# All four chunks of the soma product laid between the groups of the span phase

## What is computed

```python
# layer 0: per-language adapter
h = relu(x @ W1 + b1); x = x + layernorm(x + h @ W2 + b2) * gamma0 + beta0
# layer 1
ctx    = causal_ema(x, tau_ctx)
wg     = sigmoid(concat([x, ctx]) @ Wg.T + bg)          # "wg", the gates
gated  = x * wg                                          # g
mod    = 0.5 + sigmoid(gelu(x @ Wn1.T + bn1) @ Wn2.T + bn2)   # 8 factors per token
traces = [causal_ema(gated * mod[d], tau[d]) for d in range(8)]
temporal = sum_d traces[d] * softmax(blend)[d]
gate = sigmoid(temporal @ Wtemp.T + btemp)
soma = gelu(x @ Wsoma.T + bsoma)                         # "soma"
out  = (soma * gate) @ Wout.T
x = x + layernorm(out) * gamma1 + beta1
```

## Time and profile before

| what | us |
|---|---|
| median of three runs | 1395.28 |
| lowest and highest of them | 1391.39, 1396.88 |
| the profiled execution, its own time | 1391.26 |
| its span in the trace | 1389.3 |
| PE busy | 1345.3 (97% of the span) |
| DVE busy | 1019.6 (73%) |
| ACT busy | 511.2 (37%) |
| POOL busy | 379.0 (27%) |
| time of the packets of q1, share of 16 DMA engines | 45.9% |

### The profile page before, as it was taken

One profiled execution on the slowest core, in us unless ns is written; L12 is line 12 of the kernel. 1 busy time (PEld: TensorE's weight loads), 2 busy tenths in 40 slices (PEclk: granted clock), 3 DMA queues, 4 the chain that ended last, 5 costly groups with the idle time before them and its releaser, 6 DMA issues.

```text
span 1389.3 us, 19545 instructions
## 1 busy us (share of the span) xinstructions
PE 1345.3 (97%) x7836; PEld 971.2 (70%) x7836; DVE 1019.6 (73%) x1499; ACT 511.2 (37%) x804; POOL 379.0 (27%) x295
## 2 busy tenths in 40 slices
PE   4799999999999999999999999999999999999998
PEld 2657768677686767768577686767868677686766
DVE  7987777786777777777786777767777786677565
ACT  3225234242523425244242433425234252433412
POOL 3614123041420504123031322304123041330202
PEclk9899999999999999999999999999999999999999
DMA  7373451826438172461715626074451825426061
GB/s 261 121 194 118 121 171 63 208 84 163 141 89 222 38 215 81 126 210 58 209 44 152 190 76 197 31 192 150 114 160 68 210 94 143 161 72 172 25 158 61
DMA packets 91483, 186.21 MB, mean 134 GB/s; under 512 B 9858, under 2 KB 14594, under 8 KB 87298
## 3 DMA queue, kind: packets, MB, share of 16 engines
q1 hardware_dynamic: 91394, 184.98, 45.9%
HBM read 134.61 MB, written 50.33 MB: 133 GB/s over the span
## 4 chain that ended last, share of the span: by engine, by line
PE 57%; DMA 12%; DVE 11%; issue 8%; ACT 3%; SPq 2%; POOL 2%; DVEq 0%; POOLq 0%
PE ring L919 40%; DMA g_blocks<-g_f 7%; PE Tp L1093 5%; DMA grep<-g_blocks 5%; DVE U L825 4%; PE ring L912 3%; PE Tp L1102 3%; SPq L331 2%; PE ring L1114 2%; PE Tp L919 1%; DVE x L755 1%; DVE V L760 1%; ACT U L500 1%; DVE g_f L834 1%; PE ring L939 1%
## 5 line engine op out<-in xcount | busy, mean ns | idle before, releaser
L825 DVE TENSOR_TENSOR U<-grep,w_qs 128x1024 f32<-128x1024 f32 x256 | 300.8, 1220 | 74.4 <-DMA grep<-g_blocks 35.7
L385 POOL TENSOR_TENSOR x<-grep,b_row 128x512 f32<-128x512 f32 x64 | 80.7, 1293 | 572.8 <-DMA grep<-in_x 572.8
L1093 PE MATMUL Tp<-U,Arep 128*32 128x256 f32 x2048 | 145.9, 386 | 6.3 <-DVE U L825 6.1
L506 ACT ACTIVATE g_f<-g_f 128x512 f32<-128x512 f32 x64 | 40.4, 632 | 270.4 <-DVE g_f L830 270.2
L399 POOL TENSOR_TENSOR grep<-grep,beta_row 128x512 f32<-128x512 f32 x64 | 80.9, 1296 | 162.1 <-DMA grep<-x_tiles 162.1
L1093 PEld LDWEIGHTS Tp<-U,Arep 128*32 128x32 f32 x2048 | 54.1, 109 | 91.9 <-issue 55.2
L919 PE MATMUL ring<-x1T_hi,Wsoma_hi 128*128 128x512 f32 x256 | 114.7, 448 | 0.0
L830 DVE TENSOR_TENSOR g_f<-ring,bg_row 128x512 f32<-128x512 f32 x64 | 44.1, 689 | 85.8 <-PE ring L919 85.7
L919 PE MATMUL ring<-seq_hi,Wtemp_hi 128*128 128x512 f32 x256 | 106.8, 417 | 0.1
L919 PE MATMUL ring<-Wg_hi,seq_hi 128*128 128x512 f32 x256 | 100.4, 392 | 6.4 <-DVE seq_lo L691 6.4
L919 PE MATMUL ring<-Wg_hi,x1T_hi 128*128 128x512 f32 x256 | 104.2, 407 | 0.0
(11 more groups left out here) (158 smaller groups left out, 2762.0 us busy)
## 6 DMA issues: line engine op xcount, KB each, us to landing
grep<-g_blocks SPq DMA_DIRECT2D x256, 256.0 KB, 4.3
grep<-in_xc SPq DMA_DIRECT2D x16, 1024.0 KB, 6.4
grep<-in_x SPq DMA_DIRECT2D x16, 1024.0 KB, 8.7
x_tiles<-x SPq DMA_DIRECT2D x16, 1024.0 KB, 7.6
g_blocks<-g_f SPq DMA_DIRECT2D x64, 256.0 KB, 4.0
grep<-x_tiles SPq DMA_DIRECT2D x16, 1024.0 KB, 4.8
out<-U SPq DMA_DIRECT2D x64, 256.0 KB, 2.0
gamma_row<-in_g SPq DMA_DIRECT2D x9, 256.0 KB, 7.2
```

What stands on the lines that cost most here:

```text
L385: nc.gpsimd.tensor_tensor(new[:, b, :], x_t[:, b, :], b2_row[:, :], ALU.add).then_inc(xb2_ready, 1)
L506: nc.scalar.activation(g[:, b, :], g[:, b, :], ACT.Sigmoid).then_inc(sig_ready, 1)
L825: V_.tensor_tensor(U[:, (n + 2) % 4, :, :], grep[b % 2][:, :, at], w_qs[:, hh, at].unsqueeze(1).to_broadcast([P, NI, HC]), ALU.mult).then_ ...
L1093: last = nc.tensor.matmul(Tp[b % 2][i * L:(i + 1) * L, at], Arep[:, b * NI + i, hh, :], U[:, (n + 2) % 4, i, :], start=(hh == 0 and c == 0 ...
```

## The change

Before, the first soma chunk was computed ahead of the gate products, with all its twelve matmuls in one piece. Now it is moved behind them, into the span phase, and the chunks take other places between the span groups. The order of the bank list and the order of ACT follow: ACT's first GELU of a tile now stands behind the four sigmoids of the gates.

```diff
@@ groups_of @@
-                order += [("soma", k, 0)] + [("wg", k, b) for b in range(NB)]
-                order += [("soma", k, 1), ("soma", k, 2), ("tt", k, 0), ("soma", k, 3)]
-                order += [("tt", k, b) for b in range(1, NB)]
+                order += [("wg", k, b) for b in range(NB)]
+                order += [("soma", k, 0), ("soma", k, 1), ("tt", k, 0), ("soma", k, 2), ("tt", k, 1), ("tt", k, 2)]
+                order += [("soma", k, 3), ("tt", k, 3)]
@@ ACT @@
-                if has_cur:
-                    soma_gelu(0)
...
                     for b in range(1, NB):
                         open_gate(b)
+                    soma_gelu(0)
                     soma_gelu(1)
@@ PE @@
                 if has_cur:
                     if k == 0:
-                        pe.wait_ge(split_lo[1], 1)
-                    soma_of(0)
-                    if k == 0:
                         pe.wait_ge(split_lo[2], 1)
...
                     within_spans(0, 0)
-                    soma_begun(1)
+                    if k == 0:
+                        pe.wait_ge(split_lo[1], 1)
+                    soma_begun(0)
                     within_spans(0, 1)
                     span_states()
+                    soma_ended(0)
+                    soma_begun(1)
+                    within_spans(1, 0)
                     soma_ended(1)
                     from_before(0)
-                    within_spans(1, 0)
-                    soma_begun(2)
                     within_spans(1, 1)
                     from_before(1)
                     within_spans(2, 0)
                     trace_by_channels(0)
-                    soma_ended(2)
+                    soma_begun(2)
                     within_spans(2, 1)
                     from_before(2)
-                    soma_begun(3)
+                    soma_ended(2)
                     within_spans(3, 0)
...
                     if has_next:
-                        soma_ended(3)
+                        soma_of(3)
                         trace_by_channels(3)
                     else:
+                        soma_begun(3)
                         trace_by_channels(3)
                         soma_ended(3)
```

## The result

| | median us | lowest to highest | runs |
|---|---|---|---|
| before | 1394.42 | 1390.38 to 1396.88 | 6 |
| changed | 1429.37 | 1426.93 to 1431.07 | 6 |

The ratio is 1.0253, with a 95% interval of 1.0231 to 1.0274. The change costs 35 us, where 26 were forecast. The profiled execution took 1427.03 us, its span is 1425.1.

The account below looks back on a forecast made before the run. The transfers, not PE, were taken to bound the span phase's end. Terms 20.4, 0.5, 2.5 and 4.5 made +27.9 us: 1419.2 on the profiled 1391.26, 1423.2 as median; the middle, 1421 us, was forecast, range 1404 to 1436.

Parts of the forecast that it names:

- my own case: Whole kernel: the summed forecast holds, 1411 to 1429 us, chance 61%.
- rival (c): PE's clock falls in the new wait ahead of the span states, in five to twelve slots: 1429 to 1440 us, 17%.
- The bound: End of the span phase belongs to the transfers, not to PE; PE's waits for U are 5.4 us in all.
- Part 1: Gates come 2.72 us earlier on PE, the sigmoid only 0.67, the store of g later: 4.5 us lost in all.
- +0.3 us for the chain in each of the 15 slots: Store of g goes out later, since POOL's fourth addition ends 0.4 us later: 4.5 us, bounds -3 to +6.
- Part 2: PE newly idles about 1.5 us ahead of the span states, waiting for the last gate.
- Part 3: Behind the last half group, twelve soma matmuls instead of six: 1.36 us in each slot, 20.4 us in all.
- 24 for 18: Soma matmuls between span states and last block, new order for old; PE arrives 1.4 us later than its lead says.
- Slot 0: In the slot without output, chunk 0 no longer runs before the wait for the context: +2.5 us.
- (a): Loads come down with the gates, DVE starts up to 2.7 us earlier, the new wait vanishes: 1388 to 1396 us, 9%.
- (b): Store of block 1, up to 1.5 us earlier, slips between the loads; 0.7 us lead per slot: 1406 us, 13%.

Follow-up runs that it names:

- x2_sp_act: Changed kernel, with the store and loads of g's first block ahead of the output stores and the first sigmoid ahead of scaling the output: 1402.5 us, ratio 1.0069.
- x1_sp: Changed kernel, with the store and loads of g's first block ahead of the four output stores in SP's queue, ACT unchanged: 1434.2 us, ratio 1.0299.
- w4_delay: Changed kernel, with ACT waiting for POOL's third residual addition before the first sigmoid of a gate: 1419.4 us, ratio 1.0162.
- w3_both: Changed kernel, with the second half of chunk 0 ahead of the span states and the first half of chunk 3 ahead of the last block: 1409.1 us.
- w1_fill: Changed kernel, with the second half of soma chunk 0 ahead of the span states instead of behind them: 1429.0 us, ratio 1.0235.
- w2_tail: Changed kernel, with the first half of chunk 3 ahead of the last block's span groups, six soma matmuls left behind them: 1422.5 us, ratio 1.0188.
- y4_early: As x2_sp_act, with the first half of chunk 3 ahead of the last block and chunk 0 ahead of the gates in slot 0: 1392.8 us.
- z1_best: As y4_early, with the new order in slot 0 too, second half of chunk 0 ahead of the span states there: 1393.1 us, ratio 0.9996.
- y5_before_early: Kernel before, with g's first store and loads ahead of the output stores, first and modulation sigmoids ahead of the scaling: 1418.3 us, ratio 1.0151.

## Why the prediction was right, and what was mis-sized

**The number.** 1429.4 us were measured for 1421 forecast, inside the range. It lies at the upper edge of what I had given my own case (1411 to 1429), where rival (c) begins (1429 to 1440). By the time alone the two could not be told apart; the rows below do it.

**The bound.** Right. The end of the phase is set by the chain of transfers; filling PE's wait changed nothing (1.0235 for 1.0253), and starting the whole chain earlier, the sigmoid, the store of g and the output stores, took 25 to 27 us away (`x2_sp_act`). Moving the first store and its loads alone was no help (`x1_sp`).

**Part 1, the lead of the gates.** Right in each step. In slot 7 the sigmoid started 0.58 us earlier behind zero (672.81 - 664.05 = 8.76, for 9.34), where 0.67 was forecast. g was ready 1.25 us earlier and not 2.72, since DVE no longer had to wait out POOL's last addition; POOL's additions grew by 0.47 us, where 0.39 was forecast; and the store was issued 0.26 us later, where 0.3 was.

**The mis-sized term.** "+0.3 us for the chain in each of the 15 slots", with +0.4 as its upper bound, measured 0.84 at the first piece of U, twice that bound. I took the landing of the store for fixed at its old 2.16 us. It took 2.33 us in most slots, and about 4 us in four, so 2.85 for 2.34 in the mean. This 0.5 us a slot, 7 us in all, is most of the 9 us by which the forecast was short. The row to look for was there: slot 13 of the kernel before, with a landing of 4.33 us, showed that this transfer had a second duration.

The Trainium skill (SBUF — State Buffer, section "SBUF: two separate sides") would have had POOL wait for a whole multiplication, 0.69 us. That one of the two waits for the other, the trace agrees: `w4_delay` gave POOL its old 5.18 us back. The price was 0.47 us, nearer to the 0.39 taken from slot 0.

**Part 2, the new wait.** Right: about 1.5 us forecast, 1.44 us measured, in 12 of the 15 slots and less in three, 20.2 us in all (some 20 forecast). It is so regular because both ends hang on DVE: PE's half group starts behind the last piece of U of block 0, and the last gate follows that piece at a fixed distance.

**Part 3, the end.** Right: +1.38 us behind the last `from_before`, for 1.36 forecast. I had called it "on the path in each slot", which is true only with the wait of part 2; `w3_both` shows that the two are one loss of 20 us, for 20.4 forecast. The count "24 for 18" of part 3 holds up to `from_before(2)`; up to the first group of the last block it is 30 for 24. The six that count are the same.

**Slot 0.** 2.5 us forecast, 2.3 measured.

**The rivals.** (a), the loads coming down with the gates, did not happen. The run that brought the loads forward took 1402.5 and not 1388 to 1396, so its price was too low as well. (b) was wrong in its mechanism: the store of block 1 went out 1.0 us earlier behind zero in most slots, but its loads in slot 7 came at 21.47 (685.52 - 664.05), where it was 21.54 before, and in the mean of the 14 slots at 21.74, for 21.00. (c), the falling clock, did not occur. In the page's slices the granted clock is 9 tenths or more from the third one on, as in the kernel before. From 1.5 us ahead of the span states to 5 us behind their start it was 1.00 in all 15 slots. The windows of the changed kernel around the span states of slots 6 and 7 (granted clock is the third number from the end):

```profile
691.00:693.40 2.40, 0.96 (x12) 0.25 (x16) 1.70 (x3) 1.89 (x2) 0.00 (x0) 1.00 0.34 102
605.50:608.50 3.00, 1.56 (x17) 0.27 (x13) 2.30 (x4) 1.91 (x2) 0.00 (x0) 1.00 0.45 131
```

PE stood still for 1.44 us in both and stayed at the upper level, 2.4 GHz, as in the third of the earlier trace rows.

## What to carry to other kernels

Work laid into another place does not help where the end of the phase belongs to another chain; it is paid for where it now stands bare. Before moving filler from one place to another, find what sets the end of the phase, and count what will be left behind it. And an engine that becomes ready earlier can take a turn from its neighbour (POOL's additions, 5.65 us for 5.18), or bring a transfer closer to another, and so make the chain later: follow its neighbours too.

## What the runs showed of the hardware

A store of 256 KB issued 0.38 us behind the last of four others landed after 2.33 us in most slots, and after 3.99 to 4.53 us in slots 4, 13 and 14 of all four runs with that spacing (the changed kernel, `w1_fill`, `w2_tail`, `w3_both`), with 2.9 to 4.4 in slot 5. Issued ahead of those stores, in `x1_sp`, it took 2.00 to 2.03 us in all 15; in four of the five other kernels with that place one landing was late, 2.9 to 3.2 us in slot 12 (`x2_sp_act`, `y4_early`, `z1_best`) and 4.31 us in slot 13 (`y5_before_early`). A wait added to one engine (ACT, in `w4_delay`) made the kernel 10 us faster.
